# A new cyclic order of all parts of a windowed-attention kernel, with separate semaphores for the two projection banks

## The reference

```python
for i in range(DEPTH):        # 6 layers
    x = attn_layer(shift_tokens(x), Wqkv[i], q_scale[i], k_scale[i], Wo[i]) + x
    x = ffn_layer(shift_tokens(x), ln_g[i], ln_b[i], W1[i], b1[i], W2[i], b2[i]) + x

def attn_layer(x, Wqkv, qs, ksc, Wo):   # 16 heads of 64, windows of 32 tokens
    q, k, v = split(x @ Wqkv)
    q, k = rotary(l2norm(q) * qs), rotary(l2norm(k) * ksc)
    return local_attention(q, k, v) @ Wo      # softmax over this window and the one before

def ffn_layer(x, g, bln, W1, b1, W2, b2):
    a, gate = split(layernorm(x) * g + bln @ W1 + b1)   # 341 columns each
    return a * gelu(gate, approximate=False) @ W2 + b2
```

## Time and profile before

| | us |
|---|---|
| median of 3 runs | 1754.73 |
| lowest, highest | 1752.4, 1757.2 |
| profiled execution, its span | 1764.5 |
| TensorE busy | 1603.1 |
| VectorE busy | 1226.0 |
| ScalarE busy | 1147.8 |
| GpSimd busy | 1002.6 |

### The profile page before, as it was taken

How to read it: one execution, slowest core, us unless ns; L and a number is a source line. 1 busy time by engine, 2 the same in 40 slices (tenths; PEclk the granted TensorE clock), 3 DMA queues, 4 the chain that set the end, 5 groups by cost and what they waited for, 6 DMA issues and landing times. The chain is left out here.

```text
span 1764.5 us, 75677 instructions
## 1 busy us (share of the span) xinstructions
PE 1603.1 (91%) x33590; PEld 1308.3 (74%) x33590; DVE 1226.0 (69%) x1912; ACT 1147.8 (65%) x2115; POOL 1002.6 (57%) x757
## 2 busy tenths in 40 slices
PE   5969899988999999999998999998999999999987
PEld 4557778777777777777787787787777777778765
DVE  7766677675767767767776776776777677677662
ACT  2246677765676776766776677676676676767644
POOL 2155566664656666655675665685566585566551
PEclk9989999998999999999999999999999999999987
DMA  3266665675566567566657656657665665665650
GB/s 129 57 168 136 156 151 131 155 182 132 126 150 155 123 154 204 139 143 154 141 135 184 167 129 152 150 128 184 164 148 133 161 143 137 157 155 123 150 123 25
DMA packets 98567, 252.96 MB, mean 143 GB/s; under 512 B 30016, under 2 KB 36288, under 8 KB 97472
## 3 DMA queue, kind: packets, MB, share of 16 engines
q1 hardware_dynamic: 98240, 248.12, 59.1%
HBM read 44.59 MB, written 2.10 MB: 26 GB/s over the span
## 5 line engine op out<-in xcount | busy, mean ns | idle before, releaser
L803 DVE SCALAR_TENSOR_TENSOR UV<-ps,veca,rope 128x512 f32<-128x512 f32 x768 | 530.7, 744 | 187.5 <-PE ps L381 163.7
L1210 POOL TENSOR_TENSOR KK<-UV 128x512 f32<-128x512 f32 x192 | 241.6, 1280 | 396.3 <-DVE UV L803 393.0
L955 ACT ACTIVATE sq<-ps 128x512 f32<-128x512 f32 (+1 forms) x400 | 228.1, 583 | 269.5 <-PE ps L381 176.8
L1210 POOL TENSOR_TENSOR Qtb<-UV 128x512 f32<-128x512 f32 x192 | 243.1, 1288 | 92.4 <-DVE UV L803 92.4
L381 PE MATMUL ps<-xh,wh 128*128 128x256 f32 x768 | 244.4, 318 | 4.4 <-DVE UV L803 2.5
L381 PEld LDWEIGHTS ps<-PT,V 64*64 64x64 f32 x12288 | 199.1, 137 | 45.0 <-issue 38.6
L1229 POOL TENSOR_TENSOR E<-E,ri 128x1024 f32<-128x1024 f32 x96 | 182.7, 1903 | 78.6 <-DVE ri L876 73.2
L381 PE MATMUL ps<-PT,V 64*64 64x32 f32 x12288 | 215.7, 222 | 8.0 <-issue 5.0
L381 PE MATMUL ps<-xh,wl 128*128 128x256 f32 x768 | 217.1, 283 | 0.9 <-issue 0.9
L381 PE MATMUL ps<-xl,wh 128*128 128x256 f32 x768 | 217.2, 283 | 0.0
L1220 POOL TENSOR_TENSOR E<-E,mx 128x1024 f32<-128x1024 f32 x96 | 182.7, 1903 | 58.6 <-DVE mx L870 58.6
(11 more groups left out here) (128 smaller groups left out, 3113.9 us busy)
## 6 DMA issues: line engine op xcount, KB each, us to landing
V<-Vs SPq DMA_DIRECT2D x672, 128.0 KB
KK<-KK SPq DMA_DIRECT2D x384, 128.0 KB
Qtb<-Qtb SPq DMA_DIRECT2D x384, 128.0 KB, 2.4
rope<-in_c_rope SPq DMA_DIRECT2D x48, 512.0 KB
raw<-in_Wqkv SPq DMA_DIRECT2D x6, 1536.0 KB, 7.8
V<-Vs SPq DMA_DIRECT2D x96, 64.0 KB
V<-V SPq DMA_DIRECT2D x96, 64.0 KB, 2.0
wo<-in_Wo SPq DMA_DIRECT2D x6, 512.0 KB
```

Source lines behind the costliest of these rows:

```text
L803: e.scalar_tensor_tensor(UV[:, p % 2, slot, :].rearrange("p (i t) -> p i t", i=2), ps[:, half, :].rearrange("p (i t) -> p i t", i=2), veca ...
L955: return e.activation(out, in_, f, **kw)
L1210: e.tensor_tensor(dst, u, v, op).then_inc(s["rot_done"], 1)
```

## The change

- SCHEDULE is new as a whole. The 111 tokens are the same parts, in another order. A suffix "-1" runs a part one iteration later, "+2" two earlier; so the step now begins with `a_v0`, and what had stood at the end of the step (c_gelu, c_h1, c_h2, c_down, c_fin, b_pt2, b_pt3, b_att2, b_att3, a_norm1, a_rot3) stands in the first part of the next one. The loop runs from -2 to N + 2, and the last additions (`tail`) are spread over three iterations.
- `proj_done`, `sq_done` and `mul_done` become one each for bank 0 (x) and bank 1 (y). A table, SQUARE_FIRST, says for which of the four projections of a bank the square comes ahead of the multiply. All who waited for the old counts wait for the new ones.
- The wait of `b_pt0` for the second `b_scale` (semaphore `e_done`) moves to `b_att0`.

The diff, cut to its core; the other hunks replace waits on the old semaphores by the same on the new ones:

```diff
@@ -54,13 +54,14 @@
 PTB, WO, NORM, FF = 4, 5, 6, 7
 
 
-SCHEDULE = """b_rcq a_mx0 a_xs+1 a_vs0 a_v0 a_v1 b_rq a_my0 a_x0 a_xh+1 b_scale0 a_rot0 a_vs1 a_y0 b_lnq b_max0 a_sqy0 b_rqt
-    b_sub0 b_s0 a_rot1 b_nrm0 a_sqx0 a_mx1 b_s1 a_my1 a_x1 a_y1 c_xb a_sqy1 a_rl c_wo w_h0 b_s2 b_sum0 b_sub1
-    a_norm0 a_xl+1 w_h1 a_sqx1 b_exp0 c_xs c_zl a_rck c_mu w_l0 b_s3 c_var b_nrm1 c_zsq a_halo a_x2 a_lnk a_rot2
-    c_rs a_rot3 a_y2 a_rh a_sqy2 b_pt0 b_pto0 b_scale1 b_pt1 c_zh b_att0 w_l2 b_max1 b_att1 a_sp0 b_pto1 a_sqx2
-    c_h0 c_zn b_exp1 a_mx2 a_sp1 a_my2 b_oto0 c_gelu0 b_sum1 b_wo a_x3 c_wl c_gelu1 a_kn0 b_pto2 c_h1 b_pt2 c_hm0
-    a_y3 a_kn1 b_xb a_mx3 a_sqy3 a_sqx3 b_pt3 c_hm1 c_wh b_att2 c_h2 a_norm1 w_h2 a_my3 c_hm2 b_att3 b_pto3 c_down
-    c_gelu2 c_fin w_l1 b_oto1""".split()
+SCHEDULE = """a_v0 c_gelu0-1 b_xb-1 c_hm0-1 a_vs0 a_norm1-1 a_rot3-1 a_v1 w_h2-1 c_h1-1 b_rcq a_vs1 b_lnq a_x0 a_xh+1 b_nrm1-1
+    b_pt2-1 b_pto2-1 a_mx0 b_pt3-1 c_gelu1-1 b_pto3-1 a_y0 b_att2-1 a_sqy0 a_sqx0 a_xl+1 a_my0 b_att3-1 c_hm1-1 w_h0
+    a_x1 a_mx1 w_l2-1 b_oto1-1 a_y1 b_rqt a_sqy1 b_s0 b_rq b_s1 a_sqx1 a_my1 w_h1 a_xs+2 a_norm0 b_scale0 c_h2-1
+    a_rot0 a_rot1 a_rck b_max0 c_wo a_lnk c_gelu2-1 a_y2 c_hm2-1 c_xb c_xs b_sub0 c_down-1 a_my2 b_exp0 c_mu a_x2
+    c_zsq a_rh a_sqx2 w_l1 a_sqy2 c_var b_sum0 b_s2 b_s3 a_mx2 a_rl c_rs c_zn b_nrm0 c_wh-1 c_wl-1 c_zh b_scale1
+    w_l0 a_sp0 a_sp1 b_pt0 b_pt1 b_pto0 a_kn0 b_att0 b_pto1 b_max1 a_kn1 b_att1 c_zl a_x3 a_halo b_oto0 a_y3 b_sub1
+    c_fin-1 a_sqy3 a_mx3 c_h0 b_exp1 a_sqx3 a_my3 b_wo b_sum1 a_rot2""".split()
+SQUARE_FIRST = ((2,), (0, 1, 3))
 LAG = {"w": 0, "a": 0, "b": 1, "c": 2}
 EARLY = """a_xs0 a_xh0 a_xl0 a_halo0 a_v0 a_vs0 a_v1 a_vs1 a_x0 a_y0 a_mx0 a_my0 a_sqy0 a_sqx0 a_rot0
     a_x1 a_y1 a_mx1 a_my1 a_sqy1 a_sqx1 a_rot1 a_norm0 a_sum0 a_rck0 a_lnk0 a_rh0 a_rl0 a_sp0 a_sp1 a_kn0 a_kn1
@@ -68,19 +69,19 @@
 
 
 def part(token):
-    name, plus = (token[:-2], 1) if token.endswith("+1") else (token, 0)
-    return name.rstrip("0123456789"), int(name[-1]) if name[-1].isdigit() else 0, LAG[token[0]] - plus
+    name, ahead = (token[:-2], int(token[-2:])) if token[-2] in "+-" else (token, 0)
+    return name.rstrip("0123456789"), int(name[-1]) if name[-1].isdigit() else 0, LAG[token[0]] - ahead
 
 
 def run(parts, tail):
 
-    for it in range(-1, N + 2):
+    for it in range(-2, N + 3):
         for name, i, lag in map(part, SCHEDULE):
             early = it == lag and name + str(i) in EARLY
             if name in parts and 0 <= it - lag < N and not early:
                 parts[name](it - lag, i)
         if it >= N:
-            for g in range(G - 2) if it == N else (G - 2, G - 1):
+            for g in (range(G - 3), (G - 3,), (G - 2, G - 1))[it - N]:
                 tail(g)
...
                     elif m and r == 0:
-                        e.wait_ge(s["sq_done"], m * 8)
+                        e.wait_ge(s["sqx_done"], m * 4)
+                        e.wait_ge(s["mulx_done"], m * 8)
                     elif m:
-                        e.wait_ge(s["mul_done"], m * 16)
+                        e.wait_ge(s["sqy_done"], m * 4)
+                        e.wait_ge(s["muly_done"], m * 8)
...
-                ins.then_inc(s["proj_done"], 1)
+                ins.then_inc(s[("projx_done", "projy_done")[half]], 1)
...
-                    e.wait_ge(s["sq_done"], m * 8 + 2 * p)
+                    e.wait_ge(s["sqx_done"], m * 4 + p)
+                    e.wait_ge(s["mulx_done"], m * 8 + 2 * p)
                 project(m, p, 0)
 
             def a_y(m, p):
 
+                if p % 2 == 0 and m % G == 0:
+                    e.wait_ge(s[LOW[KB + p // 2]], m // G + 1)
                 if p == 0:
                     e.wait_ge(s["vs_done"], m * 4 + 4)
                 elif p == (3 if m else 2):
                     e.wait_ge(s["khat_done"], m * 2 + 2)
                 else:
-                    e.wait_ge(s["mul_done"], m * 16 + 4 * p)
+                    e.wait_ge(s["sqy_done"], m * 4 + p)
+                    e.wait_ge(s["muly_done"], m * 8 + 2 * p)
                 project(m, p, 1)
 
...
             def a_norm(m, side):
 
-                e.wait_ge(s["sq_done"], m * 8 + 4 * side + 4)
+                e.wait_ge(s["sqx_done"], m * 4 + 2 * side + 2)
+                e.wait_ge(s["sqy_done"], m * 4 + 2 * side + 2)
...
-                    if i == 0 and h == 1:
-                        e.wait_ge(s["e_done"], n * C + C)
...
             def b_att(n, i):
 
                 c, heads = i // 2, range(i % 2 * HQ, i % 2 * HQ + HQ)
+                if i == 0:
+                    e.wait_ge(s["e_done"], n * C + C)
                 e.wait_ge(s["pts_done"], n * 4 + i + 1)
...
+            def tables_of(m, p):
 
                 if p == 0:
                     e.wait_ge(s["tab_in"], m * 16 + 16)
                 if p == 0 and m % G == 0:
                     e.wait_ge(s["veca_in"], m // G * 16 + 16)
+
+            def a_mx(m, p):
+
+                tables_of(m, p)
                 if m or p >= 2:
                     e.wait_ge(s["rot_done"], m * 8 + 2 * p - 2)
-                e.wait_ge(s["proj_done"], m * 8 + 2 * p + 1)
+                e.wait_ge(s["projx_done"], m * 4 + p + 1)
+                if p in SQUARE_FIRST[0]:
+                    e.wait_ge(s["sqx_done"], m * 4 + p + 1)
                 multiply(m, p, 0)
 
             def a_my(m, p):
 
-                e.wait_ge(s["sq_done"], m * 8 + 2 * p + 1)
+                tables_of(m, p)
+                if m or p >= 2:
+                    e.wait_ge(s["rot_done"], m * 8 + 2 * p - 2)
+                e.wait_ge(s["projy_done"], m * 4 + p + 1)
+                if p in SQUARE_FIRST[1]:
+                    e.wait_ge(s["sqy_done"], m * 4 + p + 1)
                 multiply(m, p, 1)
...
             def a_sqy(m, p):
 
-                e.wait_ge(s["proj_done"], m * 8 + 2 * p + 2)
+                e.wait_ge(s["projy_done"], m * 4 + p + 1)
+                if p not in SQUARE_FIRST[1]:
+                    e.wait_ge(s["muly_done"], m * 8 + 2 * p + 2)
                 if m or p >= 2:
                     e.wait_ge(s["norm_done"], m * 2 + p // 2)
-                act(sq[:, p % 2, 1, :], ps[:, 1, :], ACT.Square).then_inc(s["sq_done"], 1)
+                act(sq[:, p % 2, 1, :], ps[:, 1, :], ACT.Square).then_inc(s["sqy_done"], 1)
 
             def a_sqx(m, p):
 
-                e.wait_ge(s["mul_done"], m * 16 + 4 * p + 2)
-                act(sq[:, p % 2, 0, :], ps[:, 0, :], ACT.Square).then_inc(s["sq_done"], 1)
+                e.wait_ge(s["projx_done"], m * 4 + p + 1)
+                if p not in SQUARE_FIRST[0]:
+                    e.wait_ge(s["mulx_done"], m * 8 + 2 * p + 2)
+                if m or p >= 2:
+                    e.wait_ge(s["norm_done"], m * 2 + p // 2)
+                act(sq[:, p % 2, 0, :], ps[:, 0, :], ACT.Square).then_inc(s["sqx_done"], 1)
 
...
-                for half, (x, y, op, count) in enumerate(((0, 2, ALU.subtract, 3), (3, 1, ALU.add, 4))):
-                    e.wait_ge(s["mul_done"], m * 16 + 4 * p + count)
+                for half, (x, y, op) in enumerate(((0, 2, ALU.subtract), (3, 1, ALU.add))):
+                    e.wait_ge(s["mulx_done"], m * 8 + 2 * p + half + 1)
+                    e.wait_ge(s["muly_done"], m * 8 + 2 * p + half + 1)
```

More of the change, by code:

```diff
@@ L235, in program @@
             tab_in w_in w1_in veca_in wo_in w2_in vecc_in whv_done whk_done whq_done wlv_done wlk_done wlq_done w1h_done w1l_done xa_done xs_done xh_done xl_done
-            vproj_done vs_done v2_in v2_halo k_in q_in proj_done sq_done mul_done rot_done norm_done rc_done ln_done r_done
+            vproj_done vs_done v2_in v2_halo k_in q_in projx_done projy_done sqx_done sqy_done mulx_done muly_done rot_done norm_done rc_done ln_done r_done
             rh_done rl_done rkb_done khat_done k_halo rqt_done rq_done s_done e_done m_done sub_done p_done rs_done
@@ L261, in weights_a @@
                         e.wait_ge(s[low], l)
-                    e.wait_ge(s["mul_done"], (l - 1) * G * 16)
+                    e.wait_ge(s["muly_done"], (l - 1) * G * 8)
                 e.dma_start(raw[:, :], a["Wqkv"][l]).then_inc(s["w_in"], 16)
@@ L288, in tables @@
                 if m >= 2:
-                    e.wait_ge(s["mul_done"], (m - 1) * 16)
+                    e.wait_ge(s["mulx_done"], (m - 1) * 8)
+                    e.wait_ge(s["muly_done"], (m - 1) * 8)
                 e.dma_start(rope[:, m % 2, :, :], a["c_rope"][m % G]).then_inc(s["tab_in"], 16)
@@ L494, in a_sp @@
                         if x == 0 and i == 0 and b == 0:
-                            e.wait_ge(s["sq_done"], m * 8 + (6 if m else 4))
+                            e.wait_ge(s["sqx_done"], m * 4 + (3 if m else 2))
+                            e.wait_ge(s["mulx_done"], m * 8 + (6 if m else 4))
                         elif x == 0 and i == 0:
-                            e.wait_ge(s["mul_done"], m * 16 + (12 if m else 8))
+                            e.wait_ge(s["sqy_done"], m * 4 + (3 if m else 2))
```

(19 more changed lines are left out.)

## The result

The changed kernel takes 2026.7 us (median of 4 runs, 2021.7 to 2037.8) against 1753.6 for the kernel before, run beside it (1747.1 to 1757.2): a ratio of 1.1556, 95% interval 1.1508 to 1.1604. It is slower by 273 us. The prediction was 1930 with a range of 1815 to 2080, so the sign and the range held; the forecast's own range ended at 1990, and the time lies between it and rival B.

The account below looks back on a forecast made before the run. TensorE was taken as the bound; a step of 31.5 + 3.3 + 2.0 + 1.0 less 0.3 gave 37.5 us against 34.0. Over 44 steps that is 154, plus 15 and 8: forecast 1930 us, range 1815 to 2080.

Parts of the forecast that it names:

- rival B: Stalls take TensorE's clock down, partly to 1.2 GHz: a step some 3 us longer, 2064 us in all; chance 0.16.
- The loads: Activation table loads on ScalarE: about 370 in place of 97, 6 added a step at 1.283 us, 7.7 us a step.
- rival A: One table load serves both Ln and Exp: 279 loads, a step of 35.2 us, 1823 us in all; chance 0.13.
- Stretch one: From the end of `a_v1`: TensorE stalls 1.9 us at `b_att2`, 1.3 before `b_att3`, 0.1 ahead of `a_x1`; sum 3.3.
- Stretch two: From the start of `a_x1`: loads around `a_lnk` and `c_gelu2` delay `c_xs`, so `c_mu` starts 2.0 us late.
- VectorE: Waits of `a_sp0`, `b_att0` and `a_y3` on VectorE: 1.0 us a step, bounds 0 and 2.
- The clock: TensorE's granted clock was expected near 1.00, with no time added for it; under 0.95 would point to rival B.
- The rival with a drain behind each load: Each added load costs 1.38 us more, 8.3 us a step, some 2300 us in all; chance 0.01.
- Rival C: ScalarE's 10.2 idle us a step take the loads: a step of 32.0 us, 1667 us in all; chance 0.05.
- The steps that end a layer: In 5 steps that split new weights, 3 copies at 1.05 us bound `w_h` and `c_wh`: some 3 us each, 15.
- The tail: End of the run, with `b_lnq` and Gelus of the last tiles: some added loads, 8 us.
- The small edits at nothing: Separate bank counters and some 10 more waits each on TensorE and VectorE: under 0.2 us a step, nothing taken.

## Why the prediction was right, and where its steps were off

- **The forecast and the range.** The sign and the mechanism, loads on the path that TensorE waits for, were right. The time is 97 us over the forecast of 1930 and outside its own range of 1870 to 1990; it is inside 1815 to 2080 because that was drawn out to rival B.
- **The loads.** Right in number (370), in place and in duration. Two loads for Ln and Exp, not one: the run with one shows what rival A's premise would have given, 1875 measured against 1823 worked out. A kept the clock at full, and the run had a clock of 0.955 and 47.7 us of issue waits.
- **Stretch one.** 1.9 and 1.3 were said, 2.03 and 1.12 measured; the 0.1 ahead of `a_x1` didn't show, and 0.34 stands ahead of `b_att0` instead.
- **Stretch two.** 2.0 was said, 1.86 to 2.04 measured, but at `c_down` and not at `c_mu`. The step that failed is "`c_down` is late by the same cause and is in it": `c_down` stands ahead of `c_mu` and needs the same `c_gelu2`, so it takes the stall first, and `c_mu` found `zs` ready. The sign given for it, TensorE waiting for `zs` some 2 us a step, didn't come (0.6 us in all); the wait for `hid` did (92.1 us).
- **VectorE.** 1.0 was taken, 0.2 (ahead of `a_sp0`) and the 0.34 found; inside the bounds.
- **The clock.** The term that failed. Without its stalls (2.03 + 1.12 + 1.86 + 0.20 + 0.34 = 5.55 us) a typical step of the change has 39.25 - 5.55 = 33.7 us of work against the 31.5 taken, 2.2 us a step. The forecast had nothing for it and expected a clock near 1.00, with under 0.95 as the sign of B; it was 0.905. Rival B had 3 us. Both parts are real at once: the stalls of the forecast and most of B's clock. In the mean over the 44 steps 5.81 us were lost, 3.5 were said.
- **The rival with a drain behind each load.** The Trainium skill ("ScalarE: Activation LUTs", What ACT_TABLE_LOAD costs) adds about 1380 ns to each. The trace disagrees here too: of the 370 loads all but the first of the run start 0.02 us behind the instruction ahead, and 324 are followed by one within 0.02 us (Ln at 1015.38, Exp's load at 1015.82).
- **Rival C.** It was wrong that ScalarE's idle time would take the loads. Its price is also what it gave for an order that needs no added loads, 1667; there the runs gave 1720 and 1731, with a clock of 0.97 and the issue waits, which it left out.
- **The steps that end a layer.** 15 us were put on them; they take 39.4 to 40.0 us, like the others. Two of the three copies of weights fall into the step that ends the layer and one into the next. That one, 1.07 us at 1011.58, lies where ScalarE would have waited for the second `a_v`, idle time that I had overlooked.
- **The tail.** 8 said; the stretch behind m = 47 is 7.0 longer.
- **The small edits at nothing.** Wrong in the old order (+70 us, measured). What they cost in the new order was not measured: every kernel of the new order, the fastest too, has the separate counters.

The forecast of 1930 is short by 97 us. That this is just the overlooked clock (2.2 x 44 = 97) is partly luck, since the 15 us of layer ends weren't there either, and the mean step is 0.5 longer than the typical one that gives the 2.2. The account of the profiled span, in us of TensorE's idle time, is: PT and `c_down` +240.4, `zs` and `c_zn` -49.0, `Qtb` -23.9, issue -12.1, the rest +3.4, in all +158.8 of idle, with +102.6 of busy.

## What to carry to other kernels

Before you move a part on ScalarE, write down its activation functions in the new order and count the changes of table, Ln against Exp among them: the same load was free in an idle place and cost 3.7 us a step for two in a critical one. Price a stall of TensorE that recurs in each step at more than its length, since the matmuls behind it run at a lower clock: taking 114 us of waits away gave 148 us of profiled span, 1.3 times, and adding 121.5 us of wait cost 166.5, 1.4 times. And test a new order with the costly activation replaced by a cheap one of the same length: it tells in one run whether the order or its table loads are at fault.

## What the runs showed of the hardware

- **The clock makes stalls dearer.** Three stalls of 2.0, 1.1 and 1.9 us a step took the mean granted clock from 0.98 to 0.905 and added 109 to 127 us to TensorE's work. Useless matmuls in the stalls made the kernel 45 us faster.
- **A load of a table starts as soon as its engine is free.** 370 loads, each 1.283 us, all but the first of the run 0.02 us behind the instruction ahead; where the next one had nothing to wait for, it followed within 0.02 us.
- **Issue waits.** Between 19 and 60 us of these kernels are short stops of TensorE for which no semaphore is shown. They go with the packets of 16 KB on the DMA queue that brings instructions. Of the 37 stops of the kernel before behind its first 100 us, 35 end 2.0 to 3.2 us after the start of such a packet (those that end at 398.09 and 403.74 follow packets at 395.36 and 401.24), and 46 of 46 in the kernel with the semaphores alone, where about one moment in five lies so behind a packet. Each kernel has some 260 of these packets, so most cause no stop. It looks like TensorE waiting for its code, but that is only argued: no run changed the amount of code alone. The stops are fewest (18.7 us) in the changed kernel with its long stalls, so they may take the place of a stall that is removed; that several quick kernels came out 20 to 30 us above what was expected of them would fit. It is a guess, and not all runs bear it out: one load for Ln and Exp has 47.7 us of them beside 132 us of stalls, the kernel before only 30.8.
